# Attention stage: reciprocals of the column sums as 128x16 by way of DRAM, in place of four 128x128 pieces

## The reference

```python
q = (x @ Wq).reshape(B, S, N_KV, GROUP, HEAD_DIM)
scores = jnp.einsum('bqkgd,bskd->bkgqs', q, k) * scale
scores = jnp.where(causal, jnp.finfo(scores.dtype).min, scores)
attn = jax.nn.softmax(scores, axis=-1)
out = jnp.einsum('bkgqs,bskd->bqkgd', attn, v)
...
x = x + _L0_attn_ref(xn, ...) + _L0_ffn_ref(xn, ...)
```

## Time and profile before

| | us |
|---|---|
| median of 3 runs | 3640.38 (3639.99 to 3648.52) |
| the profiled execution | 3644.07, its span 3642.0 |
| one group of stage B (the transposes of L1482 start 1550.4 to 3347.6, 15 of them) | 128.4 |
| stage B, from the first block's copy to the last (L1354) | 1447.0 to 3458.7 |
| last L1482 (step 37 of group 14) to the last copy of stage B: 3 steps and the whole last group, which has no pieces | 111 |

### The profile page before, as it was taken

How to read it: one execution, slowest core, us unless ns; L and a number is a source line. 1 busy time by engine, 2 the same in 40 slices (tenths; PEclk the granted TensorE clock), 3 DMA queues, 4 the chain that set the end, 5 groups by cost and what they waited for, 6 DMA issues and landing times. The chain is left out here.

```text
span 3642.0 us, 56595 instructions
## 1 busy us (share of the span) xinstructions
PE 3547.0 (97%) x19904; PEld 2213.6 (61%) x19904; DVE 2363.1 (65%) x5390; ACT 1629.3 (45%) x3347; POOL 2058.3 (57%) x1592
## 2 busy tenths in 40 slices
PE   7999999999997999999999999999999999999999
PEld 5888888888875555555555555555555555554387
DVE  6455555554543445877787787778778777876244
ACT  3232222222221113656566565666656566666711
POOL 0333323323332222877877787787778778778700
PEclk9999999999998999999999999999999999999999
DMA  5333333332238995102202211220221121020086
GB/s 175 102 110 101 101 110 101 101 113 97 101 122 231 286 316 147 44 24 56 50 14 58 53 32 35 56 50 13 56 54 34 35 53 43 23 68 12 19 303 241
DMA packets 228173, 340.55 MB, mean 94 GB/s; under 512 B 65088, under 2 KB 75968, under 8 KB 227968
## 3 DMA queue, kind: packets, MB, share of 16 engines
q1 hardware_dynamic: 197232, 307.77, 27.7%
q0 software_dynamic: 17920, 12.82, 1.7%
q10 hardware_dynamic: 12816, 17.33, 1.3%
HBM read 217.15 MB, written 120.35 MB: 93 GB/s over the span
## 5 line engine op out<-in xcount | busy, mean ns | idle before, releaser
L1390 ACT ACTIVATE prb<-sps 128x512 f32<-128x512 f32 (+3 forms) x2481 | 1155.1, 540 | 734.0 <-PE sps L1500 694.5
L1413 DVE TENSOR_REDUCE mx<-mps 128x1 f32<-128x512 f32 x1440 | 939.9, 681 | 161.5 <-PE mps L1477 161.4
L1325 POOL TENSOR_TENSOR rows<-rows,prb 128x1024 f32<-128x1024 f32 x372 | 881.8, 2394 | 0.0
L396 POOL DMA_INDIRECT tab_s<-pay,slot x384 | 378.0, 984 | 732.7 <-DVE tokf L694 481.0
L1416 DVE CUSTOM_DVE_ANT_0 mps<-mps,bias 128x256 f32<-128x256 f32 (+1 forms) x960 | 489.5, 523 | 212.3 <-PE mps L1477 212.0
L1518 PE MATMUL ops<-prb,vst 128*32 128x512 f32 (+3 forms) x5120 | 598.7, 539 | 6.0 <-POOL prb L1310 4.4
L1319 POOL TENSOR_TENSOR rows<-prb 128x1024 f32<-128x1024 f32 x192 | 455.1, 2392 | 151.6 <-ACT prb L1390 151.6
L1477 PE MATMUL mps<-x_lo,w_lo 96*128 96x512 f32 (+2 forms) x1280 | 487.4, 387 | 8.9 <-DVE mx L1413 3.3
L1500 PE MATMUL sps<-w_hi,x_hi 97*128 97x512 f32 (+2 forms) x1280 | 483.0, 389 | 9.8 <-ACT prb L1390 8.0
L1500 PE MATMUL sps<-w_lo,x_lo 97*128 97x512 f32 (+2 forms) x1201 | 447.4, 389 | 5.9 <-ACT prb L1390 5.9
L751 PE MATMUL acc<-x_hi,w_hi 128*128 128x512 f32 x1088 | 430.2, 395 | 6.0 <-DVE qk_lo L596 6.0
(11 more groups left out here) (178 smaller groups left out, 4256.6 us busy)
## 6 DMA issues: line engine op xcount, KB each, us to landing
wgu<-in_e_gu SPq DMA_DIRECT2D x24, 1408.0 KB, 9.2
rows<-in_x SPq DMA_DIRECT2D x16, 1024.0 KB
xn_s<-rows SPq DMA_DIRECT2D x16, 1024.0 KB, 5.1
y_sb<-in_x SPq DMA_DIRECT2D x16, 1024.0 KB
q_hi_s<-qk_hi SPq DMA_DIRECT2D x16, 1024.0 KB
q_lo_s<-qk_lo SPq DMA_DIRECT2D x16, 1024.0 KB
base<-y_sb SPq DMA_DIRECT2D x16, 1024.0 KB
w_hi<-q_hi_s SPq DMA_DIRECT2D x64, 256.0 KB, 4.4
```

The costliest lines, as they stand in the source:

```text
L396: nc.gpsimd.indirect_dma_start(t["tab"], bass.IndirectOffsetOnAxis(ap=slot[:, i, k:k + 1], axis=0), pay[:, i, k, :], None, bounds_check=E ...
L1325: nc.gpsimd.tensor_tensor(acc4, acc4, prb[:, (2 * n + pr) % RP], ALU.add).then_inc(add_done, 1)
L1390: nc.scalar.activation(prb[:, (2 * k + h // 2) % RP, h % 2, q0:CH], bank(bg, GROUP * k + h)[:, q0:CH], ACT.Exp, scale=SCALE).then_inc(exp_ ...
L1413: V.tensor_reduce(mx[:, h * NKT + qt, j:j + 1], mps[:, n % R, 0:wr], AX.X, ALU.max).then_inc(mred_done, 1)
```

## The change

For a block, SP now writes the four different rows of `den` (one partition of each head, 1x512) to a DRAM scratch `den_s`, waits, and reads the 2048 sums back as 128x16 (`dsm`). DVE makes one reciprocal of 128x16 (`rsm`). SP writes that to `rec_s`, waits, and reads each head's 512 values into its 32 partitions of `rden` (four DMAs). `normalize` on POOL waits for these instead of for DVE. DVE's reciprocal moves to the step lasts+7, `normalize` to lasts+10 (for the last block of a group: steps 6 and 9 of the next group) and behind that step's selects. The lowering by 400 in `work` is gone. On SP the order of stores and of the new DMAs is written out in `blocks`; the loads of the next keys and queries stand behind the third block's store as before. The last block of all stays as it was, in stage C.

```diff
@@ stage_b
+        EL = GROUP * CH // P
+        dsm = two("dsm", [P, EL])
+        rsm = two("rsm", [P, EL])
...
+        INVERTED, SCALED = LAG + 5, LAG + 8
...
-        for k in range(M1):
-            if any(k - LAG - 1 - part in lasts for part in range(NT)) or LAG <= k < LAG + NT:
-                work[k] -= 400
...
+            def denominators(n):
+                q = n % JC % 2
+                sp.wait_ge(den_done, n + 2)
+                for h in range(GROUP):
+                    sp.dma_start(t["den"][q, h:h + 1], den[q][HD * h:HD * h + 1, :]).then_inc(den_out, 16)
+                sp.wait_ge(den_out, 16 * GROUP * (n + 1))
+                sp.dma_start(dsm[q][:], t["den"][q].rearrange("h (c e) -> (h c) e", e=EL)).then_inc(dsm_in, 16)
+            def reciprocals(n):
+                q = n % JC % 2
+                sp.wait_ge(rsm_done, n + 1)
+                sp.dma_start(t["rec"][q].rearrange("h (c e) -> (h c) e", e=EL), rsm[q][:]).then_inc(rec_out, 16)
+                sp.wait_ge(rec_out, 16 * n + 16)
+                for h in range(GROUP):
+                    sp.dma_start(rden[q][HD * h:HD * (h + 1), :],
+                                 t["rec"][q, h:h + 1].to_broadcast([HD, CH])).then_inc(rden_in, 16)
+            def blocks(i, p):
+                n = (2 * i + p) * JC
+                if n:
+                    denominators(n - 1)
+                    reciprocals(n - 1)
+                denominators(n)
+                if n:
+                    store((n - 1) // JC // 2, (n - 1) // JC % 2, JC - 1)
+                reciprocals(n)
+                store(i, p, 0)
+                for j in range(1, JC - 1):
+                    denominators(n + j)
+                    reciprocals(n + j)
+                    store(i, p, j)
...
@@ normalize
-                pool.wait_ge(rden_done, NT * (bg * JC + j + 1))
+                pool.wait_ge(rden_in, 16 * GROUP * (bg * JC + j + 1))
...
-                    if k - LAG - NT - 1 in lasts:
-                        normalize(bg, lasts.index(k - LAG - NT - 1))
-                    if prev and k == LAG + NT:
-                        normalize(bg - 1, JC - 1)
...
+                    if k - SCALED in lasts:
+                        normalize(bg, lasts.index(k - SCALED))
+                    if prev and k == SCALED - 1:
+                        normalize(bg - 1, JC - 1)
...
@@ invert
-                if part == 0:
-                    dve.wait_ge(den_done, bg * JC + j + 2)
-                cols = slice(part * P, (part + 1) * P)
-                V.reciprocal(rden[j % 2][:, cols], den[j % 2][:, cols]).then_inc(rden_done, 1)
+                dve.wait_ge(dsm_in, 16 * (bg * JC + j + 1))
+                V.reciprocal(rsm[j % 2][:], dsm[j % 2][:]).then_inc(rsm_done, 1)
```

More of the change, by code:

```diff
@@ L1185, in stage_b @@
             att[n] for n in ("qk_in", "v_in", "c_in", "c_done", "m_done", "mred_done"))
-        att_out, att_done, rden_done, den_done = (car[n] for n in ("att_out", "att_done", "rden_done", "den_done"))
+        att_out, att_done, den_done = (car[n] for n in ("att_out", "att_done", "den_done"))
+        den_out = sem("den_out")
+        dsm_in = sem("dsm_in")
+        rsm_done = sem("rsm_done")
+        rec_out = sem("rec_out")
+        rden_in = sem("rden_in")
         s_done = sem("s_done")
@@ L1268, in _ @@
                 for p in range(2):
-                    for j in range(JC - 1):
-                        store(i, p, j)
+                    blocks(i, p)
                     for c in range(JC):
@@ L1276, in _ @@
                     load_v(sp, t, att, i + 1, p)
-                    store(i, p, JC - 1)
             sp.dma_start(wo[:], t["w_o"].rearrange("(k p) n -> p k n", p=P)).then_inc(car["wo_in"], 16)
-            for j in range(JC):
-                store(BG // 2 - 1, 0, j)
+            blocks(BG // 2 - 1, 0)
             sp.wait_ge(s_done, (BG - 1) * NU)
@@ L1283, in _ @@
                          ).then_inc(car["a_ld0"], 16)
-            for j in range(JC - 1):
-                store(BG // 2 - 1, 1, j)
+            blocks(BG // 2 - 1, 1)
         @block.gpsimd
@@ L1421, in negate, with invert @@
                 V.tensor_reduce(neg[:], mx[:], AX.X, ALU.max, negate=True).then_inc(mred_done, 1)
-            def invert(bg, j, part):
-                if part == 0:
-                    dve.wait_ge(den_done, bg * JC + j + 2)
-                cols = slice(part * P, (part + 1) * P)
-                V.reciprocal(rden[j % 2][:, cols], den[j % 2][:, cols]).then_inc(rden_done, 1)
+            def invert(bg, j):
+                dve.wait_ge(dsm_in, 16 * (bg * JC + j + 1))
+                V.reciprocal(rsm[j % 2][:], dsm[j % 2][:]).then_inc(rsm_done, 1)
             def group(bg, p, nxt, prev=True):
@@ L1446, in group @@
                             negate(bg + 1)
[L1447 to L1451, removed]
+                    if k - INVERTED in lasts:
+                        invert(bg, lasts.index(k - INVERTED))
+                    if prev and k == INVERTED - 1:
+                        invert(bg - 1, JC - 1)
             group(0, 0, True, prev=False)
@@ L1661, in _ @@
         def _(pool):
-            pool.wait_ge(rden_done, NT * (LAST + 1))
+            pool.wait_ge(rden_done, NT)
             nc.gpsimd.tensor_tensor(out[LAST % 2], num[LAST % 2], rden[LAST % 2], ALU.mult).then_inc(att_done, 1)
@@ L1773, in scratch @@
             "k_hi": dram("k_hi_s", [B, 1, P, S], F32), "k_lo": dram("k_lo_s", [B, 1, P, S], F32),
+            "den": dram("den_s", [2, GROUP, CH], F32), "rec": dram("rec_s", [2, GROUP, CH], F32),
             "tab": dram("tab_s", [E * CAP, 2], U32), "att": dram("att_s", [B, NKV, P, S], F32)}
```

## The result

The changed kernel takes 3671.35 us (median of 4 runs, 3664.39 to 3674.51) against 3640.38 us (4 runs too): a ratio of 1.0076, 95% interval 1.0064 to 1.0089. It is slower by 0.8%, where the prediction had said faster by 0.4% and had ended its range at 3655. The profiled execution took 3664.39 us, the shortest of the four.

The account below looks back on a forecast made before the run. PE sets the pace, and only its waits for DVE could shrink: 1.1 us a group in 15 groups, 16 us, so 3640.4 - 16 = 3624 us. The range, 8 in 10, was 3606 to 3655.

Parts of the forecast that it names:

- The sum for DVE: In a group with pieces, PE's lost time behind DVE was to shrink by 1.1 us, 16 us over 15 groups.
- the lumps: DVE's 0.944 us reciprocals, which delay PE's piece loads: losses of 0.13 us at step 6 and 0.53 at step 15.
- the fifth piece that leaves step 10: Step 10 goes from 5 pieces to 4 without the lowering by 400; a PE loss of 0.26 us was to go.
- the even deal: Pieces dealt without the lowering by 400; held to gain 0.3 us a group where the long reciprocals are gone.
- The loads of pieces: Sign: PE's weight loads for pieces wait for DVE by about 15 us less in 13.8 groups.
- Two signs named beforehand: DVE busy near 89 in 128 us of a steady group; SP's issues with 32 row copies not much over 0.47 us.
- The chain: The added DMAs out and back, 2.0 us a hop, were to stay hidden; for block 0, slack 2.9 us over three hops.
- The rival of the late chain: Block 0's sums return after DVE's step 10 if hops exceed 3.1 us; whole above 3651 us, chance 0.16.
- The pieces of 64 B: Two hops have 128 pieces of 64 B; at 0.5 ns a piece, a cost of 0.06 us.
- SP's loads: Next keys and queries load later, at about step 35, near ACT's small DMA; 0.6 us a group if cover is lost.
- the slack of 1.1 us: Spare time between the landing of ACT's small DMA, after 2.6 us, and PE's need of it at the group's end.
- The rebalanced pieces: The same 160 pieces and columns, with 31 for 25 in steps 3 to 9, were to cost PE nothing.

Follow-up runs that it names:

- e4: The kernel before, with each part of a reciprocal cut from 128 to its first 4 columns, same places and same deal of pieces: 3625.78 us.
- e1: The changed kernel, with SP issuing the first two parts of the next keys and queries ahead of the third block's store: 3628.28 us, ratio 0.9962.
- e6: e1 with the lowering by 400 in the deal of pieces kept as before: 3628.45 us, ratio 0.9966.
- e5: e4 with the lowering by 400 in the deal of pieces also taken out: 3630.35 us, ratio 0.9964.
- e3: The kernel before, with the lowering by 400 taken out of the deal and the reciprocals left at 4 x 128 columns: 3720.51 us, ratio 1.0217.
- e7: The changed kernel, with SP holding the third part of the loads until ACT's small DMA has landed: 3627.51 us, ratio 0.9962.
- e2: The kernel before, with the first two parts of the loads held so that all three are issued together: 3708.22 us, ratio 1.0181.

## Why the prediction was wrong

**The sum for DVE was right.** It said 1.1 us a group: some 0.8 by the lumps, and 0.26 by the fifth piece that leaves step 10, which is the deal. e4 gives 1.0 for the lumps, e1 0.9 for the whole change without the bunched loads. The split was wrong in its second half: the even deal brought nothing (e6 against e1) or cost 0.25 (e5 against e4), and that the sum still came out is in part luck. The lumps gave more than foretold at the steps 15 (0.7 for 0.53) and 6 (0.25 for 0.13); step 10 did get 0.3 us shorter by the deal (e5 against e4), but other steps paid for it. The loads of pieces waited for DVE by 13.6 us less in 13.8 groups, with 15 foretold (after: 47.0 + 37.5 + 48.3 + 36.7 = 169.5):

```profile
L1511 PEld LDWEIGHTS mps<-x_lo,w_lo 96*128 96x128 f32 x1095 | 207.4, 190 | 117.9 <-DVE mx L1450 47.0 <-DVE mx L1453 37.5 <-issue 3.4
L1511 PEld LDWEIGHTS mps<-x_hi,w_hi 96*128 96x128 f32 x1088 | 205.0, 189 | 118.3 <-DVE mx L1450 48.3 <-DVE mx L1453 36.7 <-issue 2.5
```

The new reciprocal took 0.243 us for the 0.25 worked out. Two signs named beforehand came as well: a steady group's DVE is busy 90.9 us in 128 (89 foretold), and SP's four DMAs with 32 copies of a row go out within 1.71 us, 0.43 each.

**The chain was right.** Hops of 1.4, 1.6 and 2.0 us for the 2.0 taken; no wait of DVE for `dsm` in a steady group. The rival of the late chain, the only slower case that had been given a chance, did not happen. The pieces of 64 B cost nothing that can be seen: the two hops that have them are the ones that landed in 1.4 and 1.6 us, where the calm row that the prediction went by has 2.0. The Trainium skill, page "DMA: Bandwidth & Descriptors", section "Specifications", wants at least 512 B for full rate; no run here shows a cost of that for 128 pieces.

**The step that failed is "SP's loads".** It named the mechanism, the later store and even the slack of 1.1 us, and it was sized by a wrong row. It took 4.3 us as the worst landing of the small DMA, from loads that had one part of 1 MB in flight, and so 0.6 us a group at most, and then left this out of both the forecast and the rivals. The text itself had the reason for more: three parts close together. By its own numbers SP issues a part in 6 x 0.47 = 2.8 us, 0.98 MB, which is 350 GB/s, while the profile of before moves 200 GB/s with the engines at 0.90 while two parts go out:

```profile
2298.00:2306.00 8.00, 8.00 (x46) 4.25 (x49) 7.44 (x18) 5.60 (x12) 8.00 (x5) 1.00 0.90 200
```

At the 211 to 240 GB/s seen after, 2.9 MB need 12 to 14 us from 2323.0, to 2335 to 2337 (the last of them landed at 2338.1); the small DMA, issued at 2333.3, lands behind them. It took 5.9 us: 3.3 us more, less the slack of 1.1, makes 2.2 us a group, or 31 us in 14 groups; that is what step 39 shows. The second term, which the prediction did not have at all, is PE's lowered clock after the wait. In the profiled execution it cost 6.6 us, in three groups. With 4 us for e1's 3628 in place of 3624 that makes 42 us, for the 40 by which this execution missed the forecast. The median of the runs lies 7 us higher, at 47 us; its clock was lower in two of four runs, so more of the same is likely, but no profile of such a run shows it.

**The rebalanced pieces "cost PE nothing"**: true only with the reciprocals gone. with them in place the same edit costs 79 us (e3).

## What to carry to other kernels

A wait or a step moved later in one engine's list also moves every DMA that is issued behind it in order: look at what these transfers will then run beside, and divide their bytes by the rate that the DMA engines reach, rather than taking a landing time from a calmer place. Where a small DMA is on the critical path, as here, issue bulk loads well ahead of it (e1) or hold them until it has landed (e7). And before an instruction is shortened, see whether the order around it was already laid out to hide it: what is hidden pays only after the rest is laid out anew.

## What I had not expected of the hardware

A DMA of 32 KB from another engine's queue took 5.9 us in the median in place of 2.6 while the DMA engines were full with 2.9 MB of SP's loads (share 0.99 to 1.06); a queue of its own did not shield it, though its data moved among the others' and not behind them all.

After 1.9 to 4.4 us of idle time PE was sometimes granted 1.2 GHz for a while (a granted clock of 0.57 in the 8 us after one wait in e2, 0.50 in 5 us in the changed kernel), and in other groups not: not after 2.93 us in the changed kernel. In e2 that added 1.9 us a group to a wait of 2.7 us.
